# Wo folded into the key-value blocks, the query scaled by its inverse normaliser, and a new order of the second pass

## The reference, cut to what matters

```python
q = feature_map((xn @ Wq + bq)).reshape(B, S, 16, 16)      # xn is the layer norm of x
k = feature_map((xn @ Wk + bk)).reshape(B, S, 16, 16)
v = (xn @ Wv + bv).reshape(B, S, 16, 16)
kv  = einsum('bkhd,bkhm->bhdm', k, v)
out = einsum('bqhd,bhdm->bqhm', q, kv)
normalizer = maximum(einsum('bqhd,bkhd->bqh', q, k), 1e-6)
out = (out / normalizer[..., None]).reshape(B, S, 256)
x = x + out @ Wo + bo
```

## Time and profile before

| | |
|---|---|
| median of three runs | 425.15 us (423.21 to 426.99) |
| the profiled execution, its own time | 424.78 us |
| its span, first to last instruction | 423.0 us |
| granted TensorE clock, mean | 0.996 of full |
| TensorE busy | 405.1 us (96%) |
| VectorE busy | 316.6 us (75%) |
| ScalarE busy | 218.6 us (52%) |
| GpSimd busy | 216.6 us (51%) |

### The profile page before, as it was taken

One profiled execution on the slowest core, in us unless ns is written; L12 is line 12 of the kernel. 1 busy time (PEld: TensorE's weight loads), 2 busy tenths in 40 slices (PEclk: granted clock), 3 DMA queues, 4 the chain that ended last, 5 costly groups with the idle time before them and its releaser, 6 DMA issues.

```text
span 423.0 us, 7750 instructions
## 1 busy us (share of the span) xinstructions
PE 405.1 (96%) x2570; PEld 339.7 (80%) x2570; DVE 316.6 (75%) x712; ACT 218.6 (52%) x383; POOL 216.6 (51%) x315
## 2 busy tenths in 40 slices
PE   8998999999999999989999999999999999999983
PEld 5777888988998898888788787887878787788852
DVE  5769976767767665746887788879878788887864
ACT  3776868768677776325434433423443343434441
POOL 3676776777677775111532455374236527514532
PEclk9999999999999999999999999999999999999998
DMA  8801111211100000120101101101110110111103
GB/s 263 248 14 50 53 52 55 77 67 52 50 0 0 2 0 2 12 93 2 34 27 55 51 6 52 53 11 44 52 53 1 51 54 2 53 52 51 52 5 107
DMA packets 22984, 20.66 MB, mean 49 GB/s; under 512 B 3398, under 2 KB 22924, under 8 KB 22924
## 3 DMA queue, kind: packets, MB, share of 16 engines
q1 hardware_dynamic: 22364, 19.40, 14.4%
q10 hardware_dynamic: 560, 0.52, 0.4%
HBM read 11.33 MB, written 8.45 MB: 47 GB/s over the span
## 4 chain that ended last, share of the span: by engine, by line
PE 59%; DVE 13%; POOL 8%; ACT 7%; issue 7%; SPq 2%; DMA 1%; DVEq 1%; POOLq 0%; ACTq 0%
PE PB L1453 7%; PE PT L1495 5%; PE PA L1453 4%; PE PB L1474 4%; PE PA L1535 4%; PE PA L1529 4%; PE PA L1530 3%; PE PT L1539 3%; ACT scratch L558 3%; PE PB L1501 3%; POOL ln_rstd L437 2%; PE PA L1464 2%; PE PG L1325 2%; POOL ln_rstd L435 2%; DVE ln_bn L788 2%
## 5 line engine op out<-in xcount | busy, mean ns | idle before, releaser
L487 POOL TENSOR_TENSOR ln_a<-ln_bn 128x4 f32<-128x4 f32 x32 | 6.6, 205 | 127.3 <-DVE ln_bn L991 127.3
L871 DVE SCALAR_TENSOR_TENSOR scratch<-scratch,PB 128x512 f32<-128x512 f32 x32 | 20.9, 683 | 36.5 <-ACT scratch L605 36.4
L459 POOL TENSOR_TENSOR xn_pair<-scratch,xn_pair 128x1024 fp32r<-128x1024 f32 x16 | 38.5, 2404 | 18.9 <-ACT xn_pair L569 18.9
L991 DVE BATCH_NORM_STATS2 ln_bn<-x_all 128x6 f32<-128x256 f32 x128 | 44.9, 413 | 0.9
L558 ACT ACTIVATE scratch<-x_all,ln_shift,ln_rstd 128x255 f32 (+1 forms) x60 | 31.1, 592 | 22.6 <-POOL ln_shift L441 22.6
L448 POOL TENSOR_TENSOR x_all<-x_all,wvo 128x1024 f32 (+1 forms) x16 | 38.6, 2410 | 0.1
L448 POOL TENSOR_TENSOR x_all<-x_all,ob_rows 128x1024 f32<-128x1024 f32 x16 | 37.8, 2361 | 0.0
L1298 PE MATMUL PB<-wk_hi,xt_hi 128*128 128x256 f32 x128 | 36.9, 288 | 0.6 <-DVE xt_lo L816 0.4
L1299 PE MATMUL PB<-wk_lo,xt_hi 128*128 128x256 f32 x128 | 36.2, 283 | 0.0
L1300 PE MATMUL PB<-wk_hi,xt_lo 128*128 128x256 f32 x128 | 36.2, 283 | 0.0
L724 ACT ACTIVATE scratch<-PA,ln_rsq 128x256 f32<-128x256 f32 x30 | 12.6, 471 | 45.6 <-PE PA L1453 40.3
(11 more groups left out here) (248 smaller groups left out, 1128.1 us busy)
## 6 DMA issues: line engine op xcount, KB each, us to landing
x_all<-n_L_attn_a_inputs_q_dram SPq DMA_DIRECT2D x15, 512.0 KB, 3.5
out_dram<-x_all SPq DMA_DIRECT2D x15, 512.0 KB, 3.2
out_dram<-x_all SPq DMA_DIRECT2D x2, 256.0 KB, 2.2
x_all<-n_L_attn_a_inputs_q_dram ACTq DMA_DIRECT2D x2, 128.0 KB, 3.0
x_all<-n_L_attn_a_inputs_q_dram SPq DMA_DIRECT2D x2, 128.0 KB, 2.7
setup<-in_L_attn_a_Wk_dram SPq DMA_DIRECT2D x1, 256.0 KB, 4.6
setup<-in_L_attn_a_Wq_dram ACTq DMA_DIRECT2D x1, 256.0 KB, 4.8
wvo<-in_L_attn_a_Wv_dram SPq DMA_DIRECT2D x1, 256.0 KB, 6.6
```

What stands on the lines that cost most here:

```text
L459: nc.gpsimd.tensor_tensor(xn_pair[:, :, 1, :], xn[g % 2], xn_pair[:, :, 0, :].bitcast(F32), ALU.subtract).then_inc(x_lo, 1)
L991: nc.vector.bn_stats(ln_bn[:, slot, t:t + 1, :], x_tile(n, t)).then_inc(bn, 1)
```

## The change

Wo no longer multiplies each group's result. Once a batch, `kvwo_product` multiplies the key-value blocks by Wo (two products of 128x256), ScalarE keeps the result (`keep_kvwo`), and a group's attention is then q times `kvwo`, which goes straight into the sum with x. The normaliser must for that be divided out of q beforehand: `n_product` makes it for 32 rows a tile (`kmask` is the stationary operand, 32 wide), `n_take` bounds it and takes its reciprocal on VectorE, a cast and `n_split` give its high and low part, `bc_product` spreads it over the features with a constant matrix `sel` (8 fp32r products of 128 columns), and `q_scale` multiplies q in `q_all` by it. These are made one and two steps ahead. t2 moves into the step of its own group, f4 goes to `PB`, and the order of the second pass changes on all engines. `wo_hi`, `wo_lo`, `o_hi`, `o_lo`, `o_tok` and their instructions are gone.

```diff
+            def kvwo_product(b, pair):
+                pe.wait_ge(kv_done, 2 * C * (b + 1))
+                pe.wait_ge(w2_loaded, 16 * 8)
+                for c in range(C):
+                    last = mm(pair[:, c, 0:D], g_sb[:, c, 0:P], wo_raw[:, c, :], start=True, stop=True)
+                last.then_inc(kvwo_mm, 1)
+            def n_product(j, n, b):
+                if j < B:
+                    pe.wait_ge(kv_done, 2 * C * (b + 1))
+                for c in range(C):
+                    for t in range(T):
+                        last = mm(PT[t * 2 * H:(t + 1) * 2 * H, 1, 0:P], kmask[:, b * C + c, :], q_all[:, n * C + c, t * P:(t + 1) * P],
+                                  start=(c == 0), stop=(c == C - 1), skip_group_check=True)
+                last.then_inc(n_mm, 1)
+            def bc_product(j, pair):
+                pe.wait_ge(n_op_done, j + 1)
+                for c in range(C):
+                    for t in range(T):
+                        last = mm(pair[:, c, t * P:(t + 1) * P], sel[:, t * C + c, :], n_op[:, :], start=True, stop=True)
+                last.then_inc(bc_mm, 1)
...
             def pass1(b, last):
-                    k_product(n, g)
+                    k_product(n, g, b)
+                    if last and g == G - 1:
+                        n_product(0, 0, 0)
...
                     if g == 0 and later_batch:
-                        pe.wait_ge(kv_done, 2 * C * b)
+                        pe.wait_ge(k_done, 2 * n + 2)
+                        kvwo_product(b - 1, PB)
...
+                    if last and g == G - 1:
+                        bc_product(0, PT)
                     g_product(n, g)
...
+            def n_take(j):
+                dve.wait_ge(n_mm, j + 1)
+                nc.vector.tensor_scalar(n_sb[:, :], PT[:, 1, 0:P], NORM_EPS, None, ALU.max).then_inc(n_taken, 1)
+                dve.wait_ge(n_taken, j + 1)
+                nc.vector.reciprocal(n_sb[:, :], n_sb[:, :]).then_inc(n_inv, 1)
+                dve.wait_ge(n_inv, 2 * j + 1)
+                nc.vector.tensor_copy(n_hi[:, :], n_sb[:, :]).then_inc(n_inv, 1)
+            def n_split(j):
+                dve.wait_ge(n_inv, 2 * j + 2)
+                ge(dve, bc_mm, j)
+                nc.vector.scalar_tensor_tensor(n_op[:, :], n_hi[:, :].bitcast(F32), minus_low[:, 0:1], n_sb[:, :],
+                                               ALU.mult, ALU.add).then_inc(n_op_done, 1)
+            def q_scale(j, n, pair):
+                dve.wait_ge(bc_mm, j + 1)
+                group = q_all[:, n * C:(n + 1) * C, :]
+                nc.vector.tensor_tensor(group, group, pair[:, :, :], ALU.mult).then_inc(q_scaled, 1)
...
             def pass1(b, last):
+                    if last and g == G - 1:
+                        dve.wait_ge(sel_ready, 2 + T + 1)
+                        n_take(0)
+                        n_split(0)
...
+                    if last and g == G - 1:
+                        q_scale(0, 0, PT)
...
             def step(g, b):
                 if runs(i):
+                    pe.wait_ge(q_scaled, i + 1)
+                    ge(pe, t2_done, C * i)
+                    for t in range(T):
+                        for c in range(C):
+                            last = mm(four(PA)[:, t, :], q_all[:, n * C + c, t * P:(t + 1) * P], kvwo[:, b * C + c, :],
+                                      start=(c == 0), stop=(c == C - 1))
+                    last.then_inc(w_mm, 1)
...
+                if runs(v):
+                    pe.wait_ge(f3_sq, v + 1)
+                    pe.wait_ge(q_scaled, min(i + 2, NG))
+                    ge(pe, f2_added, v + 1 if v < NG - 1 and not runs(j) else 0)
+                    pe.wait_ge(t2_done, C * min(i, NG))
+                    down(PB if v < NG - 1 else PA, h3, f4_mm)
```

## The result

The changed kernel takes 440.35 us (median of 4 runs, 439.05 to 441.43), the kernel before 425.08 in the same comparison: ratio 1.036, 95% interval 1.030 to 1.041. It is slower, on the side that was forecast and inside the range of 417 to 447, but above the 426 to 438 that the forecast had for itself, and twice as far from the kernel before as the 432 that was forecast (15.3 us, not 6.9).

A forecast was written before the change was run, and what follows sets the result against it. PE was taken to bound the second pass. Terms +2.6, +4.4, +1.0, +1.0, -0.7, +1.7 and -3.3 summed to +6.7, giving 432 us against 425.15; the forecast's own range was 426 to 438, with rivals 417 to 447.

The forecast's parts named there:

- What bounds the kernel: Second pass: PE is the bound, busy 132.81 of 133.33 us; only work taken off PE gains, if no wait replaces it.
- The plain step: Second-pass step without chain work: 13.1 us in place of 13.45, a gain of 0.35 where PE alone offers 0.94.
- The edges: Pass 1's Wo products +2.6, its last group +4.4; step 0 +1.0, steps 1 and 2 +1.0; steps 14, 15 and end -3.3.
- the wait ahead of BC(0): Last group of pass 1: PE idle 2.7 us until n_split(0) is done, then BC 0.95; g_product begins 4.4 later.
- +4.8, less 9 x 0.35, +1.7: Steps 5 to 13: chain costs 17.1 us over plain steps against 12.3 before, +4.8; less plain-step gains, net +1.7.
- (C): Rival: DVE's cast and n_split collide with POOL's row add, some 1.0 us in 13 steps, 445 us; chance 0.12.
- 17.5: The end, behind steps 14 and 15: 17.5 us, within 43.2 for that whole stretch against 46.53 before.
- (A): Rival: PE stays the bound and the new waits hide, in plain steps, ahead of BC(0) and in the chain: 417 us; chance 0.2.
- (B): Rival: BC runs at the rate of the old query products, 2.0 us, making a step 1.0 longer: 447 us; chance 0.18.

The follow-up runs named there:

- The filled idle time: Changed kernel with eleven unneeded TensorE products put into the idle time ahead of BC(0) in the first pass's last group: 438.54 us, ratio 1.031.
- the links moved: Changed kernel with step 13's four DVE chain operations, ending in the 128x256 tensor_scalar, moved ahead of the scaled sum: 434.03 us, ratio 1.020.
- BC(0) moved: Changed kernel with BC(0) moved from ahead of the last group's g_product to between its k_hi and k_lo products: 437.41 us, ratio 1.029.
- four mends of order: Changed kernel; BC(0) inside g_product, step 13's DVE operations earlier, chain slots behind h2s and f3 or h2s ahead of scaled sum in chosen steps: 427.41 us, ratio 1.006.
- h2s first: Changed kernel, every step: h2s product ahead of scaled sum and DVE's first chain slot, PE's second chain slot behind f3: 440.94 us, ratio 1.036.
- the chain late: Changed kernel, every step: DVE's first chain slot moved behind the h2s product, PE's second chain slot behind f3: 435.94 us, ratio 1.025.
- the control: Kernel before, unchanged except POOL's second-pass row add issued as four one-tile instructions: 425.72 us, ratio 1.002.

## Why the prediction was right in kind and wrong in size

**What bounds the kernel: right.** PE is the bound, and a change gives time only if no wait takes the place of the work. PE did give up work, 238.6 us busy from step 0 to the end before, 232.0 after, some of that at the lower clock; waits took more than that back.

**The plain step: right.** 13.10 against 13.1, and the path to it within 0.1: f4 starts 6.11 behind W (6.2 forecast), f3 9.64 (9.70). By its parts: W 3.27 (3.46 forecast), BC 1.03 (0.95), which cancel in part; N 0.58 with a tenth lost on f3 ahead of it and on f2 behind it (0.77 in all, as forecast), f1 and the wait for `q_scale` 1.81 (1.79), f3's wait 0.25 (0.42). The reciprocal of 128 columns takes 0.95, as worked out from two narrower ones.

**The edges: right.** The Wo products and the wait ahead of BC(0) together came to 7.22 against 7.0; steps 0 to 2 to 1.4 against 2.0; steps 14 and 15 gained 3.4 against 2.6. That the first agrees to 0.2 is in part luck: BC(0) starts between 174.4 and 176.8 in the six executions that have this first pass. The wait itself, forecast at 2.7, was 2.56 to 2.58 in all six.

**The first failing step: the chain steps 5 to 13, "+4.8, less 9 x 0.35, +1.7".** Measured +8.1. The method, a piece of chain ahead of h2s costs what it lasts, was right: in six of the nine steps the excess over 13.1 was forecast within about 0.4. It was the durations that were wrong. The sum took 0.41 and a hand-over for each 128x256 piece of DVE, from rows in which no POOL add ran. So it put step 13 at 1.9 over 13.1, and it came to 6.8; step 8 came to 2.3 where 1.4 was forecast, and step 11 to 2.1 where 1.1 was. The cause is rival (C) at another place: it was put on the cast and `n_split` of the plain steps, with a chance of 0.12. There it didn't happen (the cast took 0.23 and `n_split` 0.34 in steps 3 and 4, and POOL's add had ended 0.1 before the cast; the prediction's own 12.8 and 12.7 have the two overlap by 0.1, though its words have them miss). It struck the chain's own SBUF-to-SBUF pieces, in step 13 ahead of h2s, and `n_split` of steps 10 and 12, which DVE makes when PE is in 11 and 13, where the prediction did say that it was likely. Step 8 met it at the softmax's subtraction. The subtraction and `n_split`, each with the row add that it meets, timelines of DVE and POOL:

```profile
310.59 1.63 DVE L1233 TENSOR_TENSOR q_all<-q_all,b_weights 128x256 f32<-128x256 f32 x1
346.66 1.31 DVE L949 SCALAR_TENSOR_TENSOR n_op<-n_hi,minus_low,n_sb 128x128 fp32r<-128x128 f32 x1
...
309.59 2.36 POOL L455 TENSOR_TENSOR x_all<-x_all,ob_rows 128x1024 f32<-128x1024 f32 x1
345.28 2.54 POOL L455 TENSOR_TENSOR x_all<-x_all,ob_rows 128x1024 f32<-128x1024 f32 x1
```

They end 0.27 and 0.15 after the add. The run with the row add in pieces takes back 4.1 in step 13, with what the clock cost there, and 0.9 each in steps 8 and 11. The prediction weighed the Trainium skill's rule (SBUF — State Buffer, "Who interferes with whom"): of a DVE and a GpSimd instruction that both need the pair of SBUF ports that the two engines share, the one that issued first keeps it for its whole length. The trace agrees: in step 13 DVE's instruction ends at 388.23, POOL's at 388.08. The same section says that a DVE instruction with at most one SBUF input, outside the two-port modes, doesn't contend with GpSimd. The trace agrees here too: the adds of f2 and W, with one operand in PSUM, took 1.20 to 1.23 throughout, and three adds of f2 stood wholly within a row add.

**The second: TensorE's clock was in no term.** The prediction counted idle time at its length. Behind the wait ahead of BC(0) the products then ran at half clock, 1.6 us more, and behind step 13's wait f3, N and f2 took 5.04 in place of 3.46. The filled idle time shows the first by itself: 2.85 in place of 4.42. For step 13 the runs without the wait show it only together with the wait (4.78 with the links moved: 3.2 of wait and some 1.6 of clock).

**The third: the end, "17.5".** It took 20.18. PE waits 0.59 for the inverse variances and 1.38 for h2s there, and in the profiled execution the clock fell behind them:

```profile
423.69 0.65 PE L1571 MATMUL PT<-ident,ln_rsq 128*128 128x128 f32 x4 [0.59 <-DVE ln_rsq L1049]
425.72 1.15 PE L1586 MATMUL PT<-scratch,ffn_weights 128*128 128x512 f32 x2 [1.38 <-DVE scratch L1095]
426.68 3.58 PE L1522 MATMUL PB<-ws,scratch 128*128 128x256 f32 x8
430.08 1.91 PE L1522 MATMUL PA<-ws,scratch 128*128 128x256 f32 x8
```

f2 takes 3.40 to the next piece, and f4 behind it shows the usual 1.91. That is 1.7 of the 2.7; where the clock stayed up, the end took 18.55 (BC(0) moved). Of the other 1.0, 0.5 is the scaled sum and a piece of chain ahead of h2s, which the number of the prediction didn't hold: with both behind h2s the end took 18.05 and f3's wait was 0.83. Where the last 0.5 lies no run shows.

**The rivals.** (A), PE stays the bound and all waits hide, is refuted by 11.3 us of waits for h2s. (B), BC at 2.0, is refuted by 1.03. (C) is told above: right as a mechanism, wrong in its place. Its 445 was nearer to the truth than the forecast, but that was luck in part: it summed a loss over 13 steps that three paid, and part of step 13's loss was the clock and the order.

Put together: the change itself, with its order of work made for it and the row add in pieces, is level with the kernel before (423.8 to 425.1). Of its 15 us the four mends of order take back 13, the row add in pieces by itself 5.6, and both 16.6; they overlap in step 13. The design's own gain is small: the plain step is 0.35 shorter, 0.64 with h2s first (12.81), and the first pass pays 2.6 for its Wo products.

## What to carry to other kernels

When a change removes work that covered a chain of small operations, price each operation of that chain with the engine that shares its port running, not by its mean, and look ahead of which product on the bounding engine it stands. Where an engine off the path holds a shared port in one long instruction, cutting it into pieces can pay without a new order; here it cost GpSimd 2.83 us in place of 2.35, on which nobody waited. Count an idle time of some microseconds on TensorE as more than its length: what runs behind it may run at half clock.

## What the runs showed of the chip

The length of an idle time alone doesn't say whether the clock falls. The granted clock went to its lower level behind step 13's 3.35 to 3.56 us in all four profiles that have that wait, behind the 2.57 ahead of BC(0) in five of six, behind 2.01 (step 13 with h2s first) and 2.03 (step 8 without the normaliser), and at the end behind 1.38 in two of the seven profiles that have that wait (the changed kernel's, and that with the row add in pieces). It stayed at 1.00 behind 1.86 (step 2), 1.73 and 1.74 (step 13 with the row add cut or in pieces), 1.96 (step 11 with h2s first), 2.35 (step 7 with the chain late) and 2.78 (the same place with h2s first). And step 8's wait of 1.6 went either way. The windows behind it, with the chain late and then with h2s first too; the third number from the end is the clock:

```profile
312.70:314.70 2.00, 1.94 (x10) 1.76 (x11) 0.97 (x2) 1.49 (x4) 0.00 (x0) 1.00 0.04 13
314.70:317.00 2.30, 2.30 (x13) 2.02 (x12) 2.03 (x4) 0.00 (x0) 0.00 (x0) 1.00 0.00 0
```

```profile
312.00:313.50 1.50, 1.36 (x5) 1.17 (x6) 1.05 (x2) 1.47 (x4) 0.00 (x0) 0.68 0.04 11
313.50:315.50 2.00, 2.00 (x6) 1.58 (x5) 0.00 (x0) 0.09 (x1) 0.00 (x0) 0.50 0.00 0
```

The kernel before is no exception: in the control's profile the clock fell to 0.50 behind a wait of 2.31 in step 0, in the profile of before, where that wait is 2.06, it stayed at 1.00 through the step. The fall may begin only when PE is at work again: in the changed kernel BC(0) ran at full clock, the products behind it at 0.53. What else decides it stays open. A wait on PE is therefore priced both ways, with and without some 1.6 us behind it; once it was 3.1.
